# An expert MLP's second layer: three 256-column products become one of 512 columns and one of 256, with a PSUM bank for each tile

## The chip, the cores and the metric

The kernel runs on one core of a Trainium2 chip. TensorE is PE in the profile, and PEld its weight loads, which overlap the products; VectorE is DVE, ScalarE is ACT, GpSimd is POOL and SyncE, which issues most transfers, is SP. The metric is the device time of the whole kernel in microseconds (us).

## The reference, cut to what matters

The network routes each of 2048 tokens to two of eight experts, adds their gated sum to x, and then puts the result through a stencil step. Routing and stencil are not touched by the change.

```python
D, E, FF, TOPK = 256, 8, 1024, 2
...
hid = jax.nn.relu(jnp.einsum('nd,edf->nef', h_flat, exp_w1) + exp_b1)
eout = jnp.einsum('nef,efd->ned', hid, exp_w2) + exp_b2
y = jnp.einsum('ned,ne->nd', eout, combine)
return x + y.reshape(x.shape)
```

## The kernel before, in words

The (token, expert) pairs are sorted by expert into tiles of 128 rows, and the tiles into 23 slots, each with one expert: slot s is a single of one tile if s % 3 is 2 and a pair of two tiles otherwise (`width`). Slots 0 to 3 and 22 are written out, the 18 between them are a loop of six slots on each engine. Weights, inputs and buffers of odd and even slots are apart (`par`).

Every fp32 operand is split into a rounded half ("hi", type fp32r) and the rest ("lo"), and a product of two operands is the sum hi*hi + hi*lo + lo*hi; PARTS lists these three. For layer 2, `hid[:, par, 0]` and `hid[:, par, 1]` are the halves of the hidden values, and `w_split[:, 1, par, 0]` and `[..., 1]` those of the weights.

A slot goes through these steps; each engine has them in a fixed order, and semaphores hold the engines together.

- POOL gathers the rows, PE transposes them (`turn`, L911), ACT and VectorE make the halves (`split_h`, `low_h` at L1255).
- ACT and VectorE make the halves of the weights (`split_w1`, `low_w1` at L1243; `split_w2` at L566, `low_w2` at L1249).
- `layer1` (L935, L937, L942) on PE into banks 0 to 3; ACT adds the bias and applies relu (L586, L589), `high` rounds (L598), `low_hid` on VectorE gives the rest (L1268, L1272); for singles VectorE first adds two partial sums (`add_halves`, L1261).
- `layer2` on PE (L964): for each tile 8 blocks of 128 hidden values, three products of 256 columns each, 24 to a tile. Both tiles of a pair share bank 4 (even slots) or 5 (odd); only the last slot puts its second tile into the other of the two.
- `finish` on VectorE copies the destinations (L1282) and adds the bias while it moves the sum to y_sb (L1291; L1287 for the last slot's first tile). POOL scatters y_sb.

The order on PE is layer1(k+1), turn(k+2), layer2(k). The order on VectorE in step k is source(k+2), finish(k-2), low_w1(k+1), the work on slot k's hidden values with low_h(k+1) between, and low_w2(k). Behind the loop VectorE first prepares the stencil's grids (L1341 to L1354), and then comes finish(20), the last slot's hidden values and weights, finish(21) and finish(22).

layer2(k) waits for its weights' and hidden halves, and for y_ok to be s-1, which finish(k-2) sets: two banks take turns. The transposes use bank 6, or 7 in slot 1.

Of the kernel before, what the change touches and what calls it, by code (L numbers as in the profile page):

```python
# [7 lines left out]
ALU = mybir.AluOpType  # L8
# [7 lines left out]
P = 128  # L16
NB, T, D = 8, 256, 256
N = NB * T
NJ = N // P
KD = D // P  # L20
E, FF, TOPK = 8, 1024, 2
S_SUB, SE, SH = 32, 64, 128
FB = FF // P
ST = 256
TB = ST // P
# [20 lines left out]
def width(s):  # L46
    return 1 if s % 3 == 2 else TB


def first_col(s):  # L50
    return ROWS + s // 3 if s % 3 == 2 else 2 * (2 * (s // 3) + s % 3)


def cols_of_parity(s):
# [66 lines left out]
def moe_then_stencil(nc, x, ids, dt, exp_w1, exp_b1, exp_w2, exp_b2, a_grid, b_grid, small, consts, out):  # L121
# [4 lines left out]
    with ctx:  # L126
        def sb(name, shape, dt_=F32):
            return ctx.enter_context(nc.sbuf_tensor(name, shape, dt_))

        def sem(name):  # L130
            return ctx.enter_context(nc.semaphore(name))

        psum = ctx.enter_context(nc.psum_tensor("psum", [P, 8, 512], F32))
        banks = [psum[:, i, :] for i in range(8)]
# [11 lines left out]
        b2_all = sb("b2_all", [P, E, D])  # L146
# [9 lines left out]
        with ExitStack() as phase:  # L156
            def own(name, shape, dt_=F32):
                return phase.enter_context(nc.sbuf_tensor(name, shape, dt_))
# [3 lines left out]
            w_split = own("w_split", [P, 2, 2, 2, 2048], F32R)  # L162
            hid = own("hid", [P, 2, 2, FB, ST], F32R)
# [3 lines left out]
            y_sb = own("y_sb", [P, 2, TB, D])  # L167
# [150 lines left out]
        pool_go = sem("pool_go")  # L318
        part_ok = sem("part_ok")
        tr_done, y_ok = sem("tr_done"), sem("y_ok")  # L320
        l2_half, y_half = sem("l2_half"), sem("y_half")
        src_ok, dst_ok = sem("src_ok"), sem("dst_ok")
        rows_in = [sem(f"rows_in{i}") for i in range(2)]
# [27 lines left out]
        def field(g):  # L351
            return FV[0] if g == 0 else x_sb[:, 4 * g:4 * g + 4, :].rearrange("p j d -> p (j d)")
# [5 lines left out]
        def at_slot(k, m):  # L358
            return k if m is None else TURNS * m + (k - TURNS)
# [4 lines left out]
        def moved(k, m):  # L364
            per = 16 * cols_of_parity(TURNS - 1)
            return 16 * cols_of_parity(k) if m is None else per * m + 16 * cols_of_parity(k) - per
# [4 lines left out]
        def column(k, m):  # L371
            per = first_col(k + TURNS) - first_col(k)
            return first_col(k) if m is None else per * m + first_col(k) - per
# [103 lines left out]
        def _(act):  # L477
# [90 lines left out]
            def split_h(k, m):  # L568
                s, par, n = at_slot(k, m), k % 2, P * width(k)
                act.wait_ge(tr_done, s + 1)  # L570
                if k >= 2:
                    act.wait_ge(l1_done, BANKS * (s - 1))
                act.activation(slot_h[:, par, 0, :, 0:n],  # L573
                               banks[7 if k == 1 else 6].rearrange("p (k n) -> p k n", k=KD)[:, :, 0:n],
                               ACT.Copy).then_inc(h_hi, 1)

            def relus(k, m, bank):
# [51 lines left out]
            split_w1(0, None, first=True)  # L629
            split_w1(1, None, first=True)  # L630
            split_h(0, None)
            for k in range(FIRST):
                step(k, None)
# [40 lines left out]
            for g in range(NPAIR):  # L674
# [3 lines left out]
                for i in range(2):  # L678
# [6 lines left out]
                    else:  # L685
                        act.wait_ge(y2_added[g], 16)
                    last = act.activation(FD[g % 2][:, 512 * i:512 * i + 512], field(g)[:, 512 * i:512 * i + 512],
                                          ACT.Copy, scale=dt_b[:, 2 * g + i:2 * g + i + 1])
# [128 lines left out]
        def _(pe):  # L817
# [69 lines left out]
            for j in range(NJ):  # L887
                last = pe.matmul(banks[3][:, 0:E], ones_bf[:, :], m_bf[:, j, :], start=(j == 0), stop=(j == NJ - 1))
# [5 lines left out]
            for t in range(TOPK * NJ):  # L894
                if t % CHUNK == 0:
                    pe.wait_ge(ohrow_ok, t // CHUNK + 1)
                for part in range(2):
                    last = pe.matmul(banks[1][:, 128:128 + NC], oh_row[:, :, t], tok[:, part, :, t],  # L898
                                     start=(t == 0 and part == 0), stop=(t == TOPK * NJ - 1 and part == 1))
            last.then_inc(perm_mm, 1)  # L900

            def turn(k, m):
                s, par = at_slot(k, m), k % 2
                bank = 7 if k == 1 else 6
                pe.wait_ge(rows_in[par], moved(k, m))
                if k >= 2:
                    pe.wait_ge(h_hi, s)
                    pe.wait_ge(h_lo, s)
                for d in range(KD):
                    for t in range(width(k)):  # L910
                        last = pe.transpose(banks[bank][:, ST * d + P * t:ST * d + P * t + P],  # L911
                                            gathered[:, par, t, P * d:P * d + P], ident)
                last.then_inc(tr_done, 1)


            PARTS = ((0, 0), (0, 1), (1, 0))
# [32 lines left out]
            def layer2(k, m, halves=False):  # L949
                s, par = at_slot(k, m), k % 2  # L950
                pe.wait_ge(w2_hi, s + 1)
                pe.wait_ge(w2_lo, s + 1)
                pe.wait_ge(hid_lo, BANKS * (s + 1))
                if k >= 2:
                    pe.wait_ge(y_ok, s - 1)
                for t in range(width(k)):
                    bank = 4 + par
                    if halves and t == 1:
                        pe.wait_ge(y_ok, s)
                        bank = 5 - par  # L960
                    n = 0
                    for blk in range(FB):
                        for h, w in PARTS:
                            last = pe.matmul(banks[bank][:, D * t:D * t + D],  # L964
                                             hid[:, par, h, blk, P * t:P * t + P],
                                             w_split[:, 1, par, w, D * blk:D * blk + D],
                                             start=(n == 0), stop=(n == 3 * FB - 1))
                            n += 1
                    if halves and t == 0:
                        last.then_inc(l2_half, 1)  # L970
                last.then_inc(l2_done, 1)

            def step(k, m):
                layer1(k + 1, m)
                turn(k + 2, m)
                layer2(k, m)

            turn(0, None)
            layer1(0, None)
            for k in range(FIRST):  # L980
                step(k, None)
            with pe.Fori(1, ROUNDS + 1) as m:
                for k in range(FIRST, FIRST + TURNS):
                    step(k, m)
            layer2(NS - 1, None, halves=True)


# [40 lines left out]
        def _(dve):  # L1028
# [223 lines left out]
            def low_h(k, m):  # L1252
                s, par, n = at_slot(k, m), k % 2, P * width(k)
                dve.wait_ge(h_hi, s + 1)
                dve.tensor_tensor(slot_h[:, par, 1, :, 0:n],  # L1255
                                  banks[7 if k == 1 else 6].rearrange("p (k n) -> p k n", k=KD)[:, :, 0:n],
                                  slot_h[:, par, 0, :, 0:n].bitcast(F32), ALU.subtract).then_inc(h_lo, 1)

            def add_halves(k, m, bank):
# [16 lines left out]
            def finish(k, m, halves=False):  # L1276
                s, par, w = at_slot(k, m), k % 2, width(k)
                e = dve.value_load(e_idx[0:1, bass.DynSlice(s, 1)], min_val=0, max_val=E - 1)
                if k >= 2:
                    dve.wait_ge(y_out[par], moved(k - 2, m))  # L1280
                at = column(k, m)
                dve.tensor_copy(dst_cur[:, par, 0:w], dst_i[:, bass.DynSlice(at, w)]).then_inc(dst_ok, 1)  # L1282
                y = banks[4 + par].rearrange("p (t d) -> p t d", t=TB)
                t0 = 0
                if halves:
                    dve.wait_ge(l2_half, 1)
                    dve.tensor_tensor(y_sb[:, par, 0:1, :], y[:, 0:1, :], b2_all[:, bass.DynSlice(e, 1), :],  # L1287
                                      ALU.add).then_inc(y_half, 1)
                    y, t0 = banks[5 - par].rearrange("p (t d) -> p t d", t=TB), 1
                dve.wait_ge(l2_done, s + 1)  # L1290
                dve.tensor_tensor(y_sb[:, par, t0:w, :], y[:, t0:w, :],  # L1291
                                  b2_all[:, bass.DynSlice(e, 1), :].broadcast_to([P, w - t0, D]),
                                  ALU.add).then_inc(y_ok, 1)

            dve.wait_ge(rows_in[0], moved(0, None))
            low_w1(0, None)
            low_h(0, None)
            dve.wait_ge(rows_in[1], moved(1, None))
            low_w1(1, None)
# [45 lines left out]
            for at, cols in ((slice(0, 4), slice(0, 4)), (slice(4, 8), slice(D - 4, D))):  # L1345
                for n, gi, dst in ((0, 3, edge_w[:, 0, 0:KD, at]), (1, 1, edge_t[:, :, at]),
                                   (2, 4, edge_w[:, 1, 0:KD, at])):
                    last = dve.tensor_tensor(dst, grid[:, gi, :, cols], ew[:, n:n + 1, at].broadcast_to([P, KD, 4]),
                                             ALU.mult)
# [4 lines left out]
            dve.tensor_scalar(gr[:, 0:2, :], gr[:, 0:2, :], 0.5, None, ALU.mult).then_inc(grids_ok, 1)  # L1354

            finish(NS - 3, None)
            for bank in range(BANKS):
                low_hid(NS - 1, None, bank)
# [114 lines left out]
```

## Time and profile before

| | |
|---|---|
| median of 3 runs | 368.86 us (368.67 to 369.31) |
| span of the profiled execution | 368.1 us (368.07) |
| PE busy | 312.2 us, 85% of the span |
| VectorE busy | 286.2 us, 78% |
| ScalarE busy | 252.8 us, 69% |
| L964 (layer 2) on PE | 936 products, 117.8 us |
| mean granted TensorE clock | 0.944 |

The span is the time from the first to the last instruction of one profiled execution, and the runs were timed apart from it. Busy shares are means over stages with different limits: routing up to about 65 us, experts up to about 310, stencil behind that. A busy PE is not a PE at its peak, since consecutive products overlap in the records: how far apart they start counts, not how long one lasts.

### The profile page before, as it was taken

The numbers are of one execution on the slowest core, as the hardware profiler recorded it, in microseconds if no ns is written. First come the engines' busy times: TensorE is split into PE (matmuls) and PEld (weight loads), VectorE is DVE, ScalarE is ACT, GpSimd is POOL, SyncE is SP. The second block draws the span as 40 slices with busy tenths as digits, with TensorE's granted clock in tenths as the row PEclk, the third lists the DMA queues.
The fourth block names the chain that finished last, engine by engine and source line by source line (L and its number), as shares of the span: only waits on it lengthen the run. The fifth ranks groups of instructions, "written<-read, shape, count | busy, mean of one in ns | idle before, by whom it ended". The sixth has DMA issues, their size and how long they took to land.

```text
span 368.1 us, 7195 instructions
## 1 busy us (share of the span) xinstructions
PE 312.2 (85%) x2304; PEld 283.9 (77%) x2304; DVE 286.2 (78%) x517; ACT 252.8 (69%) x463; POOL 160.1 (44%) x114
## 2 busy tenths in 40 slices
PE   1757314789999999999999999999999996099996
PEld 1646314689999999999999999999999996034342
DVE  4988791688878878877886887887788692599993
ACT  2659014398899789789889978978988861197112
POOL 1445303152555654553554565455355414066540
PEclk9999855699999999999999999999999999579999
DMA  7902433894777875875877777576574400786513
GB/s 276 362 2 88 142 126 127 282 347 146 276 271 251 286 244 171 280 245 187 275 263 267 257 277 247 173 265 233 189 275 148 151 4 29 244 249 129 121 57 115
DMA packets 49780, 74.31 MB, mean 202 GB/s; under 512 B 3293, under 2 KB 40543, under 8 KB 49632
## 3 DMA queue, kind: packets, MB, share of 16 engines
q1 hardware_dynamic: 45056, 62.13, 49.6%
q0 software_dynamic: 4368, 11.54, 10.5%
q10 hardware_dynamic: 336, 0.39, 0.3%
q8 instruction: 10, 0.16, 0.2%
q14 instruction: 10, 0.08, 0.1%
HBM read 63.56 MB, written 9.31 MB: 198 GB/s over the span
## 4 chain that ended last, share of the span: by engine, by line
PE 72%; DVE 15%; DMA 6%; issue 2%; POOL 2%; ACT 1%; SPq 0%; DVEq 0%; POOLq 0%
PE psum L964 31%; PE psum L942 24%; PE psum L990 6%; PE psum L935 5%; PE psum L911 2%; DMA x_sb<-in_x_dram 2%; PE psum L937 2%; DMA raw_b<-in_L_cond_exp_w_dram 2%; PE psum L898 1%; DVE st L1072 1%; DMA t_y<-y_rows 1%; DVE z L1062 1%; POOL rs L722 1%; DVE t_b0f L1406 1%; PE psum L858 1%
## 5 line engine op out<-in xcount | busy, mean ns | idle before, releaser
L739 POOL DMA_INDIRECT gathered<-h_rows,src_cur x40 | 78.6, 1965 | 123.5 <-DVE src_cur L1238 66.1
L964 PE MATMUL psum<-w_split,hid 128*128 128x256 f32 x936 | 117.8, 285 | 0.2 <-issue 0.2
L964 PEld LDWEIGHTS psum<-w_split,hid 128*128 128x128 f32 x936 | 113.7, 192 | 0.3 <-issue 0.3
L942 PE MATMUL psum<-slot_h,w_split 128*128 128x256 f32 x768 | 96.5, 286 | 3.0 <-DVE slot_h L1255 3.0
L942 PEld LDWEIGHTS psum<-slot_h,w_split 128*128 128x128 f32 x768 | 94.7, 194 | 3.5 <-issue 3.5
L1249 DVE TENSOR_TENSOR w_split<-raw_b,w_split 128x2048 fp32r<-128x2048 f32 x23 | 52.7, 2293 | 22.3 <-ACT w_split L566 21.3
L589 ACT ACTIVATE relu<-psum,b_cur 128x256 f32<-128x256 f32 x128 | 53.6, 488 | 13.2 <-PE psum L942 10.9
L1243 DVE TENSOR_TENSOR w_split<-raw_a,w_split 128x2048 fp32r<-128x2048 f32 x23 | 52.5, 2282 | 8.1 <-DMA gathered<-h_rows,src_cur 7.0
L598 ACT ACTIVATE hid<-relu 128x512 fp32r<-128x512 f32 (+1 forms) x92 | 50.9, 588 | 9.6 <-DVE relu L1261 9.6
L752 POOL DMA_INDIRECT y_rows<-y_sb,dst_cur x39 | 43.1, 1106 | 27.1 <-issue 11.4
L1272 DVE TENSOR_TENSOR hid<-relu,hid 128x512 fp32r<-128x512 f32 x64 | 42.0, 687 | 10.0 <-ACT hid L598 9.4
L566 ACT ACTIVATE w_split<-raw_b 128x2048 fp32r<-128x2048 f32 x23 | 44.6, 1938 | 3.6 <-DMA raw_b<-in_L_cond_exp_w_dram 3.6
L559 ACT ACTIVATE w_split<-raw_a 128x2048 fp32r<-128x2048 f32 x23 | 44.7, 1945 | 2.6 <-DMA raw_a<-in_L_cond_exp_w_dram 2.6
L935 PE MATMUL psum<-slot_h,w_split 128*128 128x256 f32 x112 | 26.3, 332 | 0.0
L937 PE MATMUL psum<-slot_h,w_split 128*128 128x128 f32 x112 | 24.9, 223 | 0.0
L586 ACT ACTIVATE relu<-psum,b_cur 128x128 f32<-128x128 f32 x56 | 17.4, 363 | 7.7 <-PE psum L937 7.1
L937 PEld LDWEIGHTS psum<-slot_h,w_split 128*128 128x128 f32 x112 | 21.5, 192 | 0.0
L935 PEld LDWEIGHTS psum<-slot_h,w_split 128*128 128x128 f32 x112 | 21.1, 189 | 0.0
L1255 DVE TENSOR_TENSOR slot_h<-psum,slot_h 128x512 fp32r<-128x512 f32 (+1 forms) x23 | 14.0, 610 | 5.8 <-ACT slot_h L573 4.6
L911 PE MATMUL psum<-cst,gathered 128*128 128x128 f32 x80 | 13.2, 282 | 5.9 <-DMA gathered<-h_rows,src_cur 5.9
L846 PE MATMUL psum<-cst,z 128*128 128x128 f32 x32 | 8.5, 429 | 10.3 <-DVE z L1062 10.3
L573 ACT ACTIVATE slot_h<-psum 128x512 fp32r<-128x512 f32 (+1 forms) x23 | 12.8, 554 | 6.3 <-PE psum L911 6.3
(167 smaller groups left out, 357.4 us busy)
## 6 DMA issues: line engine op xcount, KB each, us to landing
raw_a<-in_L_cond_exp_w_dram SPq DMA_DIRECT2D x23, 1024.0 KB
raw_b<-in_L_cond_exp_w_dram SPq DMA_DIRECT2D x23, 1024.0 KB
t_y<-y_rows SPq DMA_DIRECT2D x6, 512.0 KB, 8.4
x_sb<-in_x_dram SPq DMA_DIRECT2D x4, 512.0 KB, 7.8
h_rows<-h_tok SPq DMA_DIRECT2D x16, 128.0 KB, 2.2
x_sb<-t_y POOLq DMA_DIRECT2D x4, 512.0 KB, 4.7
out_dram<-t_out SPq DMA_DIRECT2D x3, 512.0 KB, 2.9
b_all<-in_L_cond_exp_b_dram SPq DMA_DIRECT2D x1, 1024.0 KB, 10.5
```

The costliest lines, as they stand in the source:

```text
L559: act.activation(w_split[:, 0, par, 0, :], w1_raw[par], ACT.Copy).then_inc(w1_hi, 1)
L566: act.activation(w_split[:, 1, par, 0, :], w2_raw[par], ACT.Copy).then_inc(w2_hi, 1)
L589: last = act.activation(relu[:, bank, i, :], banks[bank][:, ST * i:ST * i + ST], ACT.Relu, bias=bias)
L598: act.activation(hid[:, par, 0, 2 * bank:2 * bank + 2, 0:n], relu[:, bank, :, 0:n], ACT.Relu if width(k) == 1 else ACT.Copy).then_inc(hid_ ...
L739: pool.indirect_dma_start(out=gathered[:, par, t, :], out_offset=None, in_=h_rows, in_offset=bass.IndirectOffsetOnAxis(ap=src_cur[:, par, ...
L752: pool.indirect_dma_start(out=y_rows, out_offset=bass.IndirectOffsetOnAxis(ap=dst_cur[:, par, t:t + 1], axis=0), in_=y_sb[:, par, t, :], i ...
L935: pe.matmul(both, w_split[:, 0, par, 0, at:at + P], slot_h[:, par, :, k, 0:P], start=(k == 0), stop=False)
L937: last = pe.matmul(both[:, 0, :], w_split[:, 0, par, 1, at:at + P], slot_h[:, par, 0, k, 0:P], start=False, stop=(k == KD - 1))
L942: last = pe.matmul(banks[bank][:, ST * (blk % 2):ST * (blk % 2) + rows], w_split[:, 0, par, w, at:at + P], slot_h[:, par, h, k, 0:rows], s ...
L964: last = pe.matmul(banks[bank][:, D * t:D * t + D], hid[:, par, h, blk, P * t:P * t + P], w_split[:, 1, par, w, D * blk:D * blk + D], star ...
L1243: dve.tensor_tensor(w_split[:, 0, par, 1, :], w1_raw[par], w_split[:, 0, par, 0, :].bitcast(F32), ALU.subtract).then_inc(w1_lo, 1)
L1249: dve.tensor_tensor(w_split[:, 1, par, 1, :], w2_raw[par], w_split[:, 1, par, 0, :].bitcast(F32), ALU.subtract).then_inc(w2_lo, 1)
```

## The change: what it does

The rounded half of hid meets both halves of the weights in one product of 512 columns, which fills a whole bank: hi*hi in its left half, hi*lo in its right. The product lo*hi of 256 columns goes into the left half. Each tile has a bank of its own: a pair of slot s takes banks 5 and 6 or 6 and 7, a single bank 5 (`out_bank`), and the transposes use bank 4, or 5 in slot 1 (`turn_bank`). layer2(k) waits for y_ok to be s, so for finish(k-1). In finish VectorE adds bias and left halves, waits for this, and adds the right halves.

```diff
+def out_bank(s):
+    return (5, 6, 5)[s % 3]
+
+
+def turn_bank(s):
+    return 5 if s == 1 else 4
...
+        y_left = sem("y_left")
...
-                bank = 7 if k == 1 else 6
+                bank = turn_bank(k)
...
-                if k >= 2:
-                    pe.wait_ge(y_ok, s - 1)
+                if k >= 1:
+                    pe.wait_ge(y_ok, s)
                 for t in range(width(k)):
-                    bank = 4 + par
-                    if halves and t == 1:
-                        pe.wait_ge(y_ok, s)
-                        bank = 5 - par
-                    n = 0
+                    out = banks[out_bank(k) + t]
                     for blk in range(FB):
-                        for h, w in PARTS:
-                            last = pe.matmul(banks[bank][:, D * t:D * t + D],
-                                             hid[:, par, h, blk, P * t:P * t + P],
-                                             w_split[:, 1, par, w, D * blk:D * blk + D],
-                                             start=(n == 0), stop=(n == 3 * FB - 1))
-                            n += 1
+                        pe.matmul(out.rearrange("p (w d) -> p w d", w=2), hid[:, par, 0, blk, P * t:P * t + P],
+                                  w_split[:, 1, par, :, D * blk:D * blk + D], start=(blk == 0), stop=False)
+                        last = pe.matmul(out[:, 0:D], hid[:, par, 1, blk, P * t:P * t + P],
+                                         w_split[:, 1, par, 0, D * blk:D * blk + D],
+                                         start=False, stop=(blk == FB - 1))
...
-                y = banks[4 + par].rearrange("p (t d) -> p t d", t=TB)
+                bias = b2_all[:, bass.DynSlice(e, 1), :]
+
+                def left(t0, t1):
+                    return dve.tensor_tensor(y_sb[:, par, t0:t1, :], psum[:, out_bank(k) + t0:out_bank(k) + t1, 0:D],
+                                             bias.broadcast_to([P, t1 - t0, D]), ALU.add)
+
+                def right(t0, t1):
+                    return dve.tensor_tensor(y_sb[:, par, t0:t1, :], y_sb[:, par, t0:t1, :],
+                                             psum[:, out_bank(k) + t0:out_bank(k) + t1, D:2 * D], ALU.add)
...
                 dve.wait_ge(l2_done, s + 1)
-                dve.tensor_tensor(y_sb[:, par, t0:w, :], y[:, t0:w, :],
-                                  b2_all[:, bass.DynSlice(e, 1), :].broadcast_to([P, w - t0, D]),
-                                  ALU.add).then_inc(y_ok, 1)
+                left(t0, w).then_inc(y_left, 1)
+                dve.wait_ge(y_left, s + 1 + t0)
+                right(t0, w).then_inc(y_ok, 1)
```

On PE, at the end of the loop and in the last slot, before:

```order
L964 MATMUL psum<-w_split,hid 128x256 [waits hid_lo,y_ok,w2_lo,w2_hi]
L964 MATMUL psum<-w_split,hid 128x256 x47
L982 REGISTER_ALU
L982 COMPARE_AND_BRANCH
L964 MATMUL psum<-w_split,hid 128x256 [waits hid_lo,y_ok,w2_lo,w2_hi]
L964 MATMUL psum<-w_split,hid 128x256 x23
L964 MATMUL psum<-w_split,hid 128x256 [waits y_ok]
L964 MATMUL psum<-w_split,hid 128x256 x23
```

The same place of the changed kernel, from the last products of the loop on:

```order
L970 MATMUL psum<-w_split,hid 128x256
L986 REGISTER_ALU
L986 COMPARE_AND_BRANCH
L968 MATMUL psum<-w_split,hid 128x512 [waits hid_lo,y_ok,w2_lo,w2_hi]
L970 MATMUL psum<-w_split,hid 128x256
```

The wait for y_ok in the middle of the last slot is gone, and the one at its start now asks for finish(21); 512 and 256 columns alternate 16 times.

On VectorE, behind the loop, from the last grid instruction to finish(21), before:

```order
L1354 TENSOR_SCALAR gr<-gr 128x1024
L1278 TENSOR_LOAD e_idx
L1278 ISA x2
L1282 COPY dst_cur<-dst_i 128x1 [waits y_out0]
L1291 ISA [waits l2_done]
L1291 TENSOR_TENSOR y_sb<-psum,b_all 128x256
L1272 TENSOR_TENSOR hid<-relu,hid 128x512 [waits hid_hi] x4
L1249 TENSOR_TENSOR w_split<-raw_b,w_split 128x2048 [waits w2_hi]
L1278 TENSOR_LOAD e_idx
L1278 ISA x2
L1282 COPY dst_cur<-dst_i 128x2 [waits y_out1]
L1291 ISA [waits l2_done]
```

The same place of the changed kernel, up to low_w2 (there L1253):

```order
L1368 TENSOR_SCALAR gr<-gr 128x1024
L1282 TENSOR_LOAD e_idx
L1282 ISA x2
L1286 COPY dst_cur<-dst_i 128x1 [waits y_out0]
L1290 ISA [waits l2_done]
L1290 TENSOR_TENSOR y_sb<-psum,b_all 128x256
L1294 TENSOR_TENSOR y_sb<-y_sb,psum 128x256 [waits y_left]
L1276 TENSOR_TENSOR hid<-relu,hid 128x512 [waits hid_hi] x4
L1253 TENSOR_TENSOR w_split<-raw_b,w_split 128x2048 [waits w2_hi]
```

Each finish has one instruction more, with a wait of its own, and none has changed its place.

## Rows read from the trace of the kernel before

**Rows 1.** Page: the chain by line, and the costliest group of PE's products

```profile
PE psum L964 31%; PE psum L942 24%; PE psum L990 6%; PE psum L935 5%; PE psum L911 2%; DMA x_sb<-in_x_dram 2%; PE psum L937 2%; DMA raw_b<-in_L_cond_exp_w_dram 2%; PE psum L898 1%; DVE st L1072 1%; DMA t_y<-y_rows 1%; DVE z L1062 1%; POOL rs L722 1%; DVE t_b0f L1406 1%; PE psum L858 1%
...
L964 PE MATMUL psum<-w_split,hid 128*128 128x256 f32 x936 | 117.8, 285 | 0.2 <-issue 0.2
```

**Rows 2.** Chain that ended last, in order of time: start us, us, what

```profile
199.93 5.76 PE psum L942 x48
```

**Rows 3.** Timeline of PE, several windows: start us, us, products merged

```profile
205.67 6.00 PE L964 MATMUL psum<-w_split,hid 128*128 128x256 f32 x48
...
227.49 3.12 PE L964 MATMUL psum<-w_split,hid 128*128 128x256 f32 x24
230.44 5.92 PE L942 MATMUL psum<-slot_h,w_split 128*128 128x256 f32 x48
...
68.80 2.55 PE L942 MATMUL psum<-slot_h,w_split 128*128 128x256 f32 x11
...
354.05 3.60 PE L990 MATMUL psum<-t_b0f,cst 128*128 128x512 f32 x8
...
359.20 3.17 PE L990 MATMUL psum<-t_u,cst 128*128 128x512 f32 x7
...
212.09 0.22 PE L937 MATMUL psum<-slot_h,w_split 128*128 128x128 f32 x1
212.15 0.33 PE L935 MATMUL psum<-slot_h,w_split 128*128 128x256 f32 x1
...
297.69 6.00 PE L964 MATMUL psum<-w_split,hid 128*128 128x256 f32 x48
303.86 5.98 PE L964 MATMUL psum<-w_split,hid 128*128 128x256 f32 x48 [0.18 <-issue]
```

**Rows 4.** Windows: us, PE busy (instructions), granted clock, DMA share, GB/s

```profile
69.00:71.00 2.00, 2.00 (x11) 0.50 1.09 353
```

**Rows 5.** Groups by form, windows 69:71 and 309.73:309.85: busy us, mean ns

```profile
L942 PE MATMUL psum<-slot_h,w_split 128*128 128x256 f32 x11 | 2.5, 415 | 0.0
...
L964 PE MATMUL psum<-w_split,hid 128*128 128x256 f32 x1 | 0.3, 279 | 0.0
```

**Rows 6.** Line L964: duration ns min/median/max, first and last start

```profile
L964 PE MATMUL psum<-w_split,hid x936: 278/283/365, 83.0 to 309.6; 128*128 128x256 f32 x188
```

**Rows 7.** Timeline of PEld in layer 1 of a single

```profile
212.09 0.19 PEld L935 LDWEIGHTS psum<-slot_h,w_split 128*128 128x128 f32 x1
212.20 0.19 PEld L937 LDWEIGHTS psum<-slot_h,w_split 128*128 128x128 f32 x1
```

**Rows 8.** Timeline of DVE, three slots: start us, us, [idle before <-releaser]

```profile
203.19 0.42 DVE L1291 TENSOR_TENSOR y_sb<-psum,b_all 128x256 f32<-128x256 f32 x1
...
222.45 0.68 DVE L1291 TENSOR_TENSOR y_sb<-psum,b_all 128x512 f32<-128x512 f32 x1
...
225.84 0.69 DVE L1272 TENSOR_TENSOR hid<-relu,hid 128x512 fp32r<-128x512 f32 x1 [0.51 <-ACT hid L598]
227.28 0.69 DVE L1272 TENSOR_TENSOR hid<-relu,hid 128x512 fp32r<-128x512 f32 x1 [0.75 <-ACT hid L598]
228.69 0.69 DVE L1255 TENSOR_TENSOR slot_h<-psum,slot_h 128x512 fp32r<-128x512 f32 x1 [0.71 <-ACT slot_h L573]
```

**Rows 9.** Timeline of DVE behind the loop

```profile
296.94 0.17 DVE L1351 TENSOR_TENSOR edge_w<-edge_w,edge_t 128x16 f32<-128x16 f32 x1
297.15 0.18 DVE L1352 COPY edge_w<-edge_w 128x32 f32<-128x32 f32 x1
...
297.57 0.69 DVE L1354 TENSOR_SCALAR gr<-gr 128x1024 f32<-128x1024 f32 x1
...
298.24 0.41 DVE L1291 TENSOR_TENSOR y_sb<-psum,b_all 128x256 f32<-128x256 f32 x1
...
301.46 2.29 DVE L1249 TENSOR_TENSOR w_split<-raw_b,w_split 128x2048 fp32r<-128x2048 f32 x1 [0.41 <-ACT w_split L566]
...
309.87 0.42 DVE L1291 TENSOR_TENSOR y_sb<-psum,b_all 128x256 f32<-128x256 f32 x1 [2.34 <-PE psum L964]
```

More of the change, by code:

```diff
@@ L573, in split_h @@
                 act.activation(slot_h[:, par, 0, :, 0:n],
-                               banks[7 if k == 1 else 6].rearrange("p (k n) -> p k n", k=KD)[:, :, 0:n],
+                               banks[turn_bank(k)].rearrange("p (k n) -> p k n", k=KD)[:, :, 0:n],
                                ACT.Copy).then_inc(h_hi, 1)
@@ L1255, in low_h @@
                 dve.tensor_tensor(slot_h[:, par, 1, :, 0:n],
-                                  banks[7 if k == 1 else 6].rearrange("p (k n) -> p k n", k=KD)[:, :, 0:n],
+                                  banks[turn_bank(k)].rearrange("p (k n) -> p k n", k=KD)[:, :, 0:n],
                                   slot_h[:, par, 0, :, 0:n].bitcast(F32), ALU.subtract).then_inc(h_lo, 1)
@@ L1286, in finish @@
                     dve.wait_ge(l2_half, 1)
-                    dve.tensor_tensor(y_sb[:, par, 0:1, :], y[:, 0:1, :], b2_all[:, bass.DynSlice(e, 1), :],
-                                      ALU.add).then_inc(y_half, 1)
-                    y, t0 = banks[5 - par].rearrange("p (t d) -> p t d", t=TB), 1
+                    left(0, 1).then_inc(y_left, 1)
+                    dve.wait_ge(y_left, s + 1)
+                    right(0, 1).then_inc(y_half, 1)
+                    t0 = 1
                 dve.wait_ge(l2_done, s + 1)
-                dve.tensor_tensor(y_sb[:, par, t0:w, :], y[:, t0:w, :],
-                                  b2_all[:, bass.DynSlice(e, 1), :].broadcast_to([P, w - t0, D]),
-                                  ALU.add).then_inc(y_ok, 1)
+                left(t0, w).then_inc(y_left, 1)
+                dve.wait_ge(y_left, s + 1 + t0)
+                right(t0, w).then_inc(y_ok, 1)
             dve.wait_ge(rows_in[0], moved(0, None))
```

## The prediction

> **What bounds the kernel now.** I read the page first: of the chain that ended last, 31% of the span are the second layer's products at L964 and 24% the first layer's at L942, both PE; PE sat idle for 0.2 us in all ahead of the 936 products of L964 [rows 1]. So the expert stage is TensorE's. In the chain, 48 products are a piece of 5.76 us, 120 ns each [rows 2], and PE's timeline shows the pieces of a stage end to end: 48 products of layer 2 from 205.67, 24 of a single from 227.49, layer 1 of the next slot from 230.44 [rows 3]. What shortens a product here shortens the kernel; what makes PE wait lengthens it. VectorE is the next engine, and its timeline tells when PE would have to wait for it.
>
> **What the change removes on PE.** A block was three products of 256 columns, 3 x 120 = 360 ns. It becomes one of 512 columns and one of 256, with one weight load less and as many columns as before (768). There are 23 slots, 7 singles of 8 blocks and 16 pairs of 16: 312 blocks. So everything hangs on how long 512 columns of this type take, which no row of before shows. From the nearest rows:
> - 256 columns are 120 ns apart. At half the granted clock (0.50, 1.2 GHz) [rows 4] 11 of them span 2.55 us [rows 3], with 415 ns for one [rows 5]: (2.55 - 0.415)/10 = 213 ns, one column per cycle. At 2.4 GHz that would be 106.7, so 13.3 ns of the 120 are something else.
> - The products of the last stage, 512 columns in two-cycle passes, are 3.60 us for 8 and 3.17 us for 7 [rows 3], 430 ns apart, some 3 above 1024 cycles. With no more surplus than that, 512 columns at one per cycle take about 216 ns: the lower bound.
> - In layer 1 of the singles a 128-column product starts at 212.09 and the next product at 212.15 [rows 3], so it holds the array 60 ns, half of 120. Read as a rate (0.47 ns per column), 512 columns take 240 ns and the change gives PE nothing: the upper bound.
> - The surplus of 13.3 ns as a fixed price of each product would make it 227; but then 128 columns would take 67, and they take 60.
> - The last product of the stage, with no weight load behind it, lasts 279 ns [rows 5], where the median is 283 [rows 6]: about 4 ns of the surplus go with the load that runs beside it. A load is about 110 ns long (two start at 212.09 and 212.20) [rows 7], so a 512-column product has one beside its first half only.
>
> I take the 128- and 256-column rows as the nearest, since they are of the same type, and let the second half go at the pace without a load: 120 for the first 256 columns, 116 for the rest, less some 2 ns for the start that is not paid twice: 234 ns. A block is then 234 + 120 = 354 against 360, a saving s of 6 ns (bounds 0 and 24).
>
> The Trainium skill ("TensorE: Matmul & The Clock Gate", Wait — 56ns, not 53.3ns?) puts consecutive warm products at N/2.4 GHz and about 2.5 ns more, 215.7 ns measured for 512 columns. By that rule a block would be 336 ns, s = 24; for 256 columns it gives 109, and the trace disagrees with 120.
>
> **What it adds on VectorE.** Each finish gets a second addition that waits for the first: 0.68 us for a pair, 0.42 for a single [rows 8], plus about 0.04 us between two dependent instructions (296.94 + 0.17 to 297.15) [rows 9]. In the steady part that is hidden by VectorE's idle time. The single's step is a train without gaps, so its extra addition and the next one's arrive together at the first pair's step, 1.5 us late; there VectorE waited 0.51, 0.75 and 0.71 us for ACT [rows 8], 1.97 in all, and the last of these three, low_h, is on time again. It ends at 228.69 + 0.69 = 229.38, and PE needs it at 230.44 [rows 3, 8]. Without that cover each late us past this last one would be PE's.
>
> **The wait that it tightens.** Layer 2 of slot k now waits for finish(k-1), not finish(k-2). On VectorE finish(k-1) stands right after low_w2(k), which layer 2 needed already. A finish that ended at 203.19 + 0.42 = 203.61 would end at 204.1, and the layer 2 that needs it starts at 205.67: 1.6 us of room. One that ended at 222.45 + 0.68 = 223.13 would end at 224.6, late and second addition together, against 227.49 [rows 3, 8]. Savings of 0.1 us per slot don't use that up. I cost the wait at nothing there.
>
> **At the end it is not hidden.** Two waits appear, one after another, on the chain that ends last.
> - Layer 2 of slot 21 started at 297.69 [rows 3]. It must now wait for finish(20), which VectorE does only after the grid work written ahead of it (its last is at 297.57): its addition runs at 298.24 for 0.41, the second ends at 298.65 + 0.04 + 0.42 = 299.11 [rows 9], and PE starts 0.11 later (as from low_w2's end, 301.46 + 2.29 = 303.75, to 303.86), at 299.2.
> - Layer 2 of slot 22 started at 303.86 [rows 3], held by low_w2 alone, since its first tile had a bank to itself. It must now wait for finish(21), which can't begin before slot 21's products are done. From the start of a pair's products to the addition behind them is 6.01 us (303.86 to 309.87) [rows 3, 9], here 6.01 - 16s: 305.21 - 16s. Then 0.69 + 0.04 + 0.69 + 0.11: PE starts at 306.74 - 16s.
> - Its own products and two additions of 0.42 follow: 306.74 + 6.01 + 0.42 + 0.04 + 0.42 = 313.63 - 32s, where before the last addition ended at 309.87 + 0.42 = 310.29 [rows 9]. low_w2, moved by 0.5 us, ends near 304 and holds nothing.
>
> All of this stands earlier by what slots 0 to 19 save, 14 pairs and 6 singles, 272 blocks; slot 20's 8 are lost, since VectorE's grid work follows layer 1 of slot 21 and not PE's later products. **The sum: +3.34 us - (272 + 32)s.** With s = 6 ns that is 3.34 - 1.82 = +1.5 us. Behind it nothing changes: scatter, loads of y and the stencil follow that last addition as before. The profiled execution's span was 368.07 us and the median of the runs is 368.86, 0.79 above; so 368.86 + 1.5 = **370.4 us**.
>
> **Rivals.**
> - *No gain on PE at all* (240 ns per 512 columns, by the exact 60 and 120): s = 0, +3.3 us, 372.2. Against it stand the 279 of the last product.
> - *A fixed surplus* (227): s = 13.3, 3.34 - 4.04 = -0.7, 368.2, no measurable change (0.2%, 0.74 us, is what a measurement of this kernel can tell). For it: the removed load is a plausible home of those ns. Against it: the 60 ns of 128 columns.
> - *The other side: the load is what stretches 256 columns.* A load takes some 110 ns and the columns 107; behind 512 columns it is hidden wholly, and the product takes 216, as the two-cycle passes suggest. s = 24 on every block, 3.34 - 7.3 = -4.0, 364.9. It decides from s = 13.5 on (a 512-column product under 226.5 ns). Against it: the last product, with no load behind it, is only 4 ns shorter, not 11. The rule of the page above is this rival's.
> - *A wait in the steady part.* If VectorE's train were 1.6 us later still, layer 2 of every first pair would stall; at half a us in each of seven turns that is 3.5 us on top, 373.9. The idle times above speak against it.
>
> **Chances.** Forecast (512 columns at 230 to 238 ns) 0.42; no gain 0.13; steady wait 0.05; fixed surplus 0.22; load hidden 0.18. So slower 0.60, same 0.22, faster 0.18. The forecast's own range is 369.2 to 371.6 (s from 10 to 2 ns). The range 366.5 to 372.8 adds the fixed surplus, with some 1.5 us below it, and the case without gain; it leaves out the hidden load and the steady wait.
>
> **What would show it.** The 512-column products last about 397 ns (234 and the 163 by which a record outlasts its pitch, 283 - 120), and the products of a pair take 5.66 us instead of 5.76. PE idles about 1.5 us ahead of slot 21's second layer and 1.8 ahead of slot 22's, released by VectorE's second addition, and nowhere else in the stage. The last addition ends 1.5 us later than 310.29. I am wrong if the 512-column records last 380 ns, if layer 2 waits for y_sb before 297 us, or if the two waits at the end are under 2.5 us together.

## The result, and the profile after

| | before | changed |
|---|---|---|
| median of 13 runs each, us | 368.86 (368.19 to 370.23) | 370.94 (369.97 to 372.61) |
| span of the profiled execution, us | 368.07 | 370.0 |
| PE busy, us | 312.2 | 309.9 |
| VectorE busy, us | 286.2 | 298.4 |

The ratio is 1.0050, with an interval of 1.0034 to 1.0066: slower, by 2.1 us. TensorE has less to do and the kernel takes longer, so there must be more idle time on TensorE; the question is what it waits for.

The page of the changed kernel, its first line, the chain by line, and the two groups that take the place of the one in [rows 1]:

```profile
span 370.0 us, 6596 instructions
...
PE psum L951 22%; PE psum L968 20%; PE psum L970 10%; PE psum L994 6%; PE psum L944 5%; PE psum L920 2%; DMA x_sb<-in_x_dram 2%; PE psum L946 2%; DMA raw_b<-in_L_cond_exp_w_dram 2%; DMA t_y<-y_rows 2%; PE psum L907 1%; DVE st L1076 1%; DVE z L1066 1%; POOL rs L731 1%; DVE t_b0f L1420 1%
...
L968 PE MATMUL psum<-w_split,hid 128*128 128x512 f32 x312 | 112.9, 404 | 3.2 <-DVE y_sb L1294 3.2
...
L970 PE MATMUL psum<-w_split,hid 128*128 128x256 f32 x312 | 87.6, 281 | 0.0
```

Layer 2 had 0.2 us of idle time ahead of its 936 products; now 3.2 us stand ahead of the 512-column ones, all ended by y_sb at L1294, VectorE's second addition. (Busy times of the two groups overlap and don't add up.) PE's waits between 72 and 316 us, the whole expert stage behind its start (us in total, times, longest), say that there are two of them:

```profile
PE psum L968 <- DVE y_sb L1294: 3.2, 2, 1.7
PE psum L951 <- DVE slot_h L1259: 0.4, 1, 0.4
```

PE's timeline has them both behind the loop, in front of slots 21 and 22; the first three rows are from the steady part:

```profile
205.33 0.40 PE L968 MATMUL psum<-w_split,hid 128*128 128x512 f32 x1
205.56 0.28 PE L970 MATMUL psum<-w_split,hid 128*128 128x256 f32 x1
205.68 0.40 PE L968 MATMUL psum<-w_split,hid 128*128 128x512 f32 x1
...
297.51 0.47 PE L968 MATMUL psum<-w_split,hid 128*128 128x512 f32 x1 [1.52 <-DVE y_sb L1294]
...
297.94 0.40 PE L968 MATMUL psum<-w_split,hid 128*128 128x512 f32 x1
...
302.79 0.40 PE L968 MATMUL psum<-w_split,hid 128*128 128x512 f32 x1
...
305.01 0.47 PE L968 MATMUL psum<-w_split,hid 128*128 128x512 f32 x1 [1.71 <-DVE y_sb L1294]
...
305.43 0.40 PE L968 MATMUL psum<-w_split,hid 128*128 128x512 f32 x1
...
309.32 0.40 PE L968 MATMUL psum<-w_split,hid 128*128 128x512 f32 x1
```

VectorE's timeline, the first three rows from the steady part (they answer to [rows 8]) and the rest from behind the loop ([rows 9]):

```profile
222.13 0.69 DVE L1290 TENSOR_TENSOR y_sb<-psum,b_all 128x512 f32<-128x512 f32 x1
222.85 0.69 DVE L1294 TENSOR_TENSOR y_sb<-y_sb,psum 128x512 f32<-128x512 f32 x1
...
227.36 0.69 DVE L1259 TENSOR_TENSOR slot_h<-psum,slot_h 128x512 fp32r<-128x512 f32 x1 [0.41 <-ACT slot_h L582]
...
295.70 0.69 DVE L1368 TENSOR_SCALAR gr<-gr 128x1024 f32<-128x1024 f32 x1
...
296.49 0.42 DVE L1290 TENSOR_TENSOR y_sb<-psum,b_all 128x256 f32<-128x256 f32 x1
296.95 0.42 DVE L1294 TENSOR_TENSOR y_sb<-y_sb,psum 128x256 f32<-128x256 f32 x1
...
303.45 0.69 DVE L1290 TENSOR_TENSOR y_sb<-psum,b_all 128x512 f32<-128x512 f32 x1 [1.39 <-PE psum L970]
304.18 0.69 DVE L1294 TENSOR_TENSOR y_sb<-y_sb,psum 128x512 f32<-128x512 f32 x1
...
311.39 0.42 DVE L1294 TENSOR_TENSOR y_sb<-y_sb,psum 128x256 f32<-128x256 f32 x1
```

Read the two timelines together. finish(20) stands behind the last grid instruction (295.70), its second addition ends at 297.37, and slot 21's products start at 297.51. finish(21) waits for slot 21's last product, its second addition ends at 304.87, and slot 22's products start at 305.01. The last addition of the stage ends at 311.81; before it ended at 310.29.

What PE gained on the way is read from the chain (start us, us, what). Layer 1 of the same slot, one turn of three slots later:

```profile
159.40 5.76 PE psum L951 x48
...
189.80 5.76 PE psum L951 x48
```

Three slots take 30.40 us. The same two pieces of the kernel before:

```profile
160.19 5.76 PE psum L942 x48
...
190.86 5.76 PE psum L942 x48
```

That is 30.67 us, so a turn's 40 blocks save 0.27 us, 6.75 ns each.

### The profile page after: what moved, and what is told of

It reads as the page before. It is cut to its first block, busy times and chain, and to the rows that moved or that the text cites. A ratio compares the mean times of both kernels' runs of the same rounds, so it can differ in the third digit from the quotient of the medians.

```text
span 370.0 us, 6596 instructions
## 1 busy us (share of the span) xinstructions
PE 309.9 (84%) x1992; PEld 266.8 (72%) x1992; DVE 298.4 (81%) x541; ACT 252.8 (68%) x463; POOL 150.8 (41%) x114
## 4 chain that ended last, share of the span: by engine, by line
PE 69%; DVE 17%; DMA 6%; issue 3%; POOL 2%; ACT 1%; SPq 1%; DVEq 0%; POOLq 0%
PE psum L951 22%; PE psum L968 20%; PE psum L970 10%; PE psum L994 6%; PE psum L944 5%; PE psum L920 2%; DMA x_sb<-in_x_dram 2%; PE psum L946 2%; DMA raw_b<-in_L_cond_exp_w_dram 2%; DMA t_y<-y_rows 2%; PE psum L907 1%; DVE st L1076 1%; DVE z L1066 1%; POOL rs L731 1%; DVE t_b0f L1420 1%
## 5 line engine op out<-in xcount | busy, mean ns | idle before, releaser
L748 POOL DMA_INDIRECT gathered<-h_rows,src_cur x40 | 63.8, 1594 | 130.2 <-DVE src_cur L1242 104.0
L968 PE MATMUL psum<-w_split,hid 128*128 128x512 f32 x312 | 112.9, 404 | 3.2 <-DVE y_sb L1294 3.2
L970 PE MATMUL psum<-w_split,hid 128*128 128x256 f32 x312 | 87.6, 281 | 0.0
L968 PEld LDWEIGHTS psum<-w_split,hid 128*128 128x128 f32 x312 | 58.6, 188 | 17.1 <-issue 3.7
L1253 DVE TENSOR_TENSOR w_split<-raw_b,w_split 128x2048 fp32r<-128x2048 f32 x23 | 52.7, 2292 | 20.2 <-ACT w_split L575 20.2
L761 POOL DMA_INDIRECT y_rows<-y_sb,dst_cur x39 | 48.7, 1248 | 31.1 <-DVE y_sb L1294 13.1
L970 PEld LDWEIGHTS psum<-w_split,hid 128*128 128x128 f32 x312 | 59.0, 189 | 0.0
L1290 DVE TENSOR_TENSOR y_sb<-psum,b_all 128x512 f32<-128x512 f32 (+1 forms) x24 | 14.0, 585 | 6.5 <-PE psum L970 6.5
```

The source lines that it names most:

```text
L748: pool.indirect_dma_start(out=gathered[:, par, t, :], out_offset=None, in_=h_rows, in_offset=bass.IndirectOffsetOnAxis(ap=src_cur[:, par, ...
L761: pool.indirect_dma_start(out=y_rows, out_offset=bass.IndirectOffsetOnAxis(ap=dst_cur[:, par, t:t + 1], axis=0), in_=y_sb[:, par, t, :], i ...
L968: pe.matmul(out.rearrange("p (w d) -> p w d", w=2), hid[:, par, 0, blk, P * t:P * t + P], w_split[:, 1, par, :, D * blk:D * blk + D], star ...
L970: last = pe.matmul(out[:, 0:D], hid[:, par, 1, blk, P * t:P * t + P], w_split[:, 1, par, 0, D * blk:D * blk + D], start=False, stop=(blk = ...
L1253: dve.tensor_tensor(w_split[:, 1, par, 1, :], w2_raw[par], w_split[:, 1, par, 0, :].bitcast(F32), ALU.subtract).then_inc(w2_lo, 1)
```

## The experiments

Every experiment is compared with runs of the kernel before on the same chip; its median there was 369.01 us for e1 to e4, 369.03 for e5 to e7 and 369.35 for e8 to e10. Since profiled spans differ by about 1 us for reasons that lie in front of and behind the experts, each trace is also read by its **expert stage**: from the start of layer 1's first product on PE to the end of the last addition on VectorE. Two profiles of one kernel (changed and e10) differ by 0.2 us in it.

| kernel | first product | last addition ends | stage, us | against before |
|---|---|---|---|---|
| before | 68.23 | 310.30 | 242.07 | |
| changed | 68.34 | 311.81 | 243.48 | +1.41 |
| e1 last slot's own banks | 68.97 | 310.53 | 241.56 | -0.51 |
| e2 finish(20) ahead of the grids | 67.48 | 310.06 | 242.58 | +0.51 |
| e3 both | 67.64 | 308.12 | 240.48 | -1.59 |
| e4 three products again | 67.38 | 312.94 | 245.56 | +3.49 |
| e5 one addition | 67.51 | 309.24 | 241.73 | -0.34 |
| e6 products grouped by width | 67.42 | 309.92 | 242.50 | +0.43 |
| e7 e3, last tile in the old form | 67.56 | 307.39 | 239.83 | -2.24 |
| e8 e7, grouped per tile | 67.43 | 306.34 | 238.92 | -3.15 |
| e9 e7, grouped over both tiles | 67.77 | 306.65 | 238.87 | -3.20 |
| e10 changed, again | 67.53 | 311.21 | 243.69 | +1.62 |

**e1: the last slot gets two banks of its own** (7 and 4), so that it needn't wait for finish(21).

```diff
+def last_bank(t):
+    return (7, 4)[t]
...
-                    pe.wait_ge(y_ok, s)
+                    pe.wait_ge(y_ok, s - 2 if halves else s)
...
-                    out = banks[out_bank(k) + t]
+                    out = banks[last_bank(t) if halves else out_bank(k) + t]
...
```

> The last slot's tiles get banks 7 and 4, which are free by then, so its products no longer wait for finish(21); the rest is the changed kernel. My theory (the loss is the two waits behind the loop, 1.5 and 1.7 us of idle PE in the trace of the changed kernel): the second wait goes and only low_w2 and slot 21's own products hold the last slot, so about 1.8 us less than the changed kernel, 369.1 us. Rival (the loss is VectorE's second additions in the steady part, and the waits at the end only stand in for others that would appear): within 0.5 us of the changed kernel's 370.9.

Measured 368.64, ratio 0.9992 (0.9976 to 1.0008). PE's waits of e1:

```profile
PE psum L972 <- DVE y_sb L1302: 1.5, 1, 1.5
PE psum L955 <- DVE slot_h L1263: 1.1, 1, 1.1
```

The longer wait is gone, the one ahead of slot 21 stays at 1.5 us, and the stage is 1.92 us shorter than the changed one, for a wait of 1.71; the other 0.2 us are within what two profiles of one kernel differ by. (The wait for slot_h is at the start of the stage, before the loop. It is 1.0 in the kernel before, 0.4 in the changed one and 0.7 in e10.)

**e2: finish(20) stands ahead of the grid work on VectorE.**

```diff
+            finish(NS - 3, None)
             dve.wait_ge(grid_in, 64)
...
-            finish(NS - 3, None)
```

> finish(20) stands ahead of the stencil's grid work on VectorE instead of behind it; the rest is the changed kernel. My theory: slot 21's products start 1.5 us earlier, but finish(21) then has to stand behind low_w2(22), which ends where it did, so slot 22's products start only about 1.4 us earlier: 369.5 us. Rival (steady part): within 0.5 us of 370.9.

Measured 368.87, ratio 1.0000 (0.9986 to 1.0014). PE's waits of e2:

```profile
PE psum L968 <- DVE y_sb L1294: 1.7, 1, 1.7
PE psum L920 <- DMA gathered<-h_rows,src_cur: 0.7, 1, 0.7
```

Now the other wait is left, 1.7 us. The stage is only 0.90 us shorter than the changed one, but that is not the edit's doing: this profile has 0.7 us of waiting for gathered rows near the stage's start, before the first product of layer 2. PE's timeline of e2 there, and below it that product in the changed kernel:

```profile
82.82 0.44 PE L920 MATMUL psum<-cst,gathered 128*128 128x128 f32 x2 [0.65 <-DMA gathered<-h_rows,src_cur]
83.02 0.48 PE L968 MATMUL psum<-w_split,hid 128*128 128x512 f32 x1
...
83.06 0.48 PE L968 MATMUL psum<-w_split,hid 128*128 128x512 f32 x1
```

From the first product of layer 2 to the last addition e2 takes 310.06 - 83.02 = 227.04 us and the changed kernel 311.81 - 83.06 = 228.75: 1.71 less, somewhat more than the wait of 1.5 that the edit removes. The +0.51 of the table is to be read with that.

**e3: e1 and e2 together.**

> Both edits, the last slot in banks 7 and 4 and finish(20) ahead of the grid work. My theory: neither wait is left, PE has at most 0.5 us of idle time ahead of the last slot (low_w2), 2.9 us less than the changed kernel, 368.0 us, so below the kernel before by about 0.9 us: what the products save (2.0 us) less the second addition that ends the stage and what low_w2 takes. Rival (steady part): no faster than the kernel before, 369 or more.

Measured 367.59, ratio 0.9958 (0.9943 to 0.9974). PE's waits of e3 have no y_sb at all:

```profile
PE psum L972 <- issue: 0.3, 1, 0.3
```

Without the two waits the change is what it looked like, a gain. Its size goes by the prediction's own terms: -304 x 6.75 ns + 0.46 for the second addition of the last finish = -1.59, and the stage has -1.59. That it fits to the last digit is luck, as two profiles of one kernel differ by 0.2 us.

**e4: the new banks, waits and additions, but three products of 256 columns**, hi*lo into the right half.

```diff
-                        pe.matmul(out.rearrange("p (w d) -> p w d", w=2), hid[:, par, 0, blk, P * t:P * t + P],
-                                  w_split[:, 1, par, :, D * blk:D * blk + D], start=(blk == 0), stop=False)
-                        last = pe.matmul(out[:, 0:D], hid[:, par, 1, blk, P * t:P * t + P],
-                                         w_split[:, 1, par, 0, D * blk:D * blk + D],
-                                         start=False, stop=(blk == FB - 1))
+                        for h, w in PARTS:
+                            last = pe.matmul(out[:, D * w:D * w + D], hid[:, par, h, blk, P * t:P * t + P],
+                                             w_split[:, 1, par, w, D * blk:D * blk + D],
+                                             start=(blk == 0 and h == 0 and w == 0), stop=(blk == FB - 1 and h == 1))
```

> The changed kernel's banks, waits and two additions, but each block again in three products of 256 columns (hi*hi and lo*hi into the left half of the bank, hi*lo into the right half). This is the sum with s = 0. My theory: the 304 blocks on the path give back 304 x 6.7 ns = 2.0 us, 372.9 us; by the forecast's own +3.3 us over the kernel before it would be 372.2. Rival (the 512-column products save nothing, and the changed kernel's loss is all there is): the same as the changed kernel, 370.9.

Measured 372.88, ratio 1.0100 (1.0080 to 1.0120). This is the cost of the change without its gain: +3.49 us in the stage, where the sum has +3.34 at s = 0. PE's waits, and the chain:

```profile
PE psum L969 <- DVE y_sb L1293: 3.2, 2, 1.7
```

```profile
159.15 5.76 PE psum L951 x48
...
189.82 5.76 PE psum L951 x48
```

The same two waits, and 30.67 us for three slots, as in the kernel before. So the new banks, waits and additions cost the loop nothing, and the 512-column product alone gives its 0.27 us per turn.

**e5: one addition per finish.**

```diff
...
-                left(t0, w).then_inc(y_left, 1)
-                dve.wait_ge(y_left, s + 1 + t0)
-                right(t0, w).then_inc(y_ok, 1)
+                left(t0, w).then_inc(y_ok, 1)
```

> The changed kernel without VectorE's second addition, so the product of hid's rounded half and the weights' low half is left out of the output; banks, products and waits are the same. My theory: the second additions cost only where PE waits for them, 0.46 us in finish(20), 0.73 in finish(21) and 0.46 in finish(22), together 1.65 us, so 369.3 us, and the steady part of three slots keeps its 30.40 us. Rival (VectorE's extra 15 us in the steady part hold PE or others up): more than 2.5 us less, below 368.4, and a shorter period.

Measured 368.41, ratio 0.9985 (0.9968 to 1.0002). Waits and chain of e5:

```profile
PE psum L968 <- DVE y_sb L1290: 1.9, 2, 1.0
```

```profile
158.61 5.76 PE psum L951 x48
...
189.01 5.76 PE psum L951 x48
```

Three slots still take 30.40 us: the second additions cost the steady part nothing. They cost at the end, where the two waits shrink from 3.2 to 1.9 us and the last finish has one addition less; the stage is 1.75 us shorter than the changed one, where the theory has 1.65. The median, 0.9 us below the theory's 369.3, stands at the edge of the rival's 368.4; what speaks against the rival is the unchanged turn.

**e6: within a tile first all eight 512-column products, then all eight of 256.**

```diff
+                    for blk in range(FB):
                         last = pe.matmul(out[:, 0:D], hid[:, par, 1, blk, P * t:P * t + P],
```

> The changed kernel with each tile's eight 512-column products first and its eight 256-column products behind them, the same work in another order. It tells where the saving of 6.7 ns per block lies. Forecast's reading (the second half of 512 columns goes without a load beside it): 512 columns 234 to 236 ns apart, 256 columns 120, a block 355, time within 0.7 us of the changed kernel. Rival 1 (a rate of 0.47 ns per column, and the alternation is what saves): 240 and 120, a block 360, about 2 us more, 372.9. Rival 2 (a fixed price of a product): 227 and 120, a block 347, about 2 us less, 368.9.

Measured 369.45, ratio 1.0014 (0.9992 to 1.0035); the stage is 0.98 us shorter than the changed one, with the 3.2 us of waits unchanged. Three slots take 30.23 us (layer 1 from 158.24 to 188.47 in its chain). The order of products alone is worth 0.17 us per turn. By the turn a block takes 349 ns, 11 less than with the old products: near rival 2's 347, and neither 355 nor 360.

**e7: e3, and the last slot's second tile has its three products of 256 columns in one half**, so that its finish needs one addition, and the semaphore between the two is not needed there.

```diff
+                        if halves and t == 1:
+                            for h, w in PARTS:
+                                last = pe.matmul(out[:, 0:D], hid[:, par, h, blk, P * t:P * t + P],
+                                                 w_split[:, 1, par, w, D * blk:D * blk + D],
+                                                 start=(blk == 0 and h + w == 0), stop=(blk == FB - 1 and h == 1))
+                            continue
...
+                if halves:
+                    left(t0, w).then_inc(y_ok, 1)
+                    return
```

> The kernel of both edits at the end (last slot in banks 7 and 4, finish(20) ahead of the grid work), and the last slot's second tile again in three products of 256 columns into one half, with one addition. My theory: the addition that ends the stage is 0.46 us shorter for 8 x 6.7 ns = 0.05 us of products, so 0.4 us less than without it, about 367.6 us, 1.3 us below the kernel before. Rival (steady part): no faster than the kernel before.

Measured 366.43, ratio 0.9926 (0.9902 to 0.9951). The stage is 0.65 us shorter than that of e3, where an addition and its start are 0.46 and 8 blocks' savings are lost. Most of the rest is not the edit's: in e7 slots 2 and 3, outside the loop, run at 347 ns a block and in e3 at 353, 0.15 us over their 24 blocks (see e10 on these two paces). The median moved by 1.2 us where the theory had 0.4; what is left of that is not accounted for.

**e8 and e9: e7, with the products grouped by width**, in e8 within a tile, in e9 over both tiles of a pair (e9's core is shown; wide(t, out) issues a tile's eight products of 512 columns, narrow(t, out) its eight of 256).

```diff
-                for t in range(width(k)):
-                    out = banks[out_bank(k) + t]
-                    for blk in range(FB):
...
+                    for t in range(width(k)):
+                        wide(t, banks[out_bank(k) + t])
+                    for t in range(width(k)):
+                        last = narrow(t, banks[out_bank(k) + t])
```

> The best kernel so far (last slot in banks 7 and 4, finish(20) ahead of the grid work, last tile in the old form) with each tile's 512-column products first and its 256-column products behind them. Theory after the grouped run (each product has a fixed surplus of 13 ns, and a 512-column product behind a 256-column one some 6 to 9 ns more): a block 347 to 348 ns instead of 353, over some 280 blocks 1.6 us less, 364.8 us. Rival (the stage is by now bound by VectorE or by the weights' loads, so faster products only wait): no change, 366.4, with waits of PE for w_split or slot_h.

> The same with the 512-column products of both tiles of a pair in a row and then the 256-column products of both. Theory (what is lost is at the change from 256 to 512 columns, some 15 ns, and there is one less to a pair): 15 pairs x 15 ns = 0.2 us less, 364.6 us, not to be told from the run with each tile apart. Rival (512 columns keep getting slower the longer they follow each other, since loads and reads of SBUF pile up): slower than that run by 0.5 us or more.

Measured 365.52, ratio 0.9904 (0.9883 to 0.9925), for e8, and 365.38, ratio 0.9886 (0.9868 to 0.9905), for e9: both beat the kernel before by some 4 us and the changed one by over 5. Against e7 the stage of e8 is 0.91 us shorter, where the theory had 1.6. Between e8 and e9 nothing can be told. PE's timeline of e9, a pair's layer 2, layer 1 of a single, and the 512-column products of the single's layer 2:

```profile
203.47 3.89 PE L971 MATMUL psum<-w_split,hid 128*128 128x512 f32 x16
207.19 2.08 PE L976 MATMUL psum<-w_split,hid 128*128 128x256 f32 x16
...
209.23 0.22 PE L950 MATMUL psum<-slot_h,w_split 128*128 128x128 f32 x1
209.29 0.34 PE L948 MATMUL psum<-slot_h,w_split 128*128 128x256 f32 x1
209.46 0.23 PE L950 MATMUL psum<-slot_h,w_split 128*128 128x128 f32 x1
209.52 0.33 PE L948 MATMUL psum<-slot_h,w_split 128*128 128x256 f32 x1
...
224.89 2.09 PE L971 MATMUL psum<-w_split,hid 128*128 128x512 f32 x8
```

The first 512-column product behind another stage holds PE for longer; with the 0.31 that it took in front of slot 21 of the changed kernel (297.51, and the 256-column product behind it at 297.82) and 0.40 for the last record, the others are (3.89 - 0.31 - 0.40)/14 = 227 ns apart. In the single the eight are (2.09 - 0.31 - 0.40)/6 = 230 ns apart. The 256-column ones are (2.08 - 0.28)/15 = 120 ns apart. Three slots take 30.19 us in e9's chain (158.55 to 188.74), 12 ns per block less than with the old products.

**e10: the changed kernel once more**, beside e8 and e9.

> The changed kernel, unaltered, beside the other two on one chip. Its expert stage, from the first transposes to the last addition, was 1.4 us longer than before in the profiled execution, while the median moved by 2.1. Theory (the 1.4 us and no more are the change's, the rest is the spread of the runs): 1.2 to 2.0 us over the kernel before, 370.4 to 371. Rival (the stage behind it has also become slower): 2.1 us or more again, with a profiled execution whose stencil stage is longer by half a us.

Measured 370.88, ratio 1.0037 (1.0021 to 1.0053), so 1.5 us slower this time, as the theory has it. (The part of the span behind the last addition is 0.4 us longer than in the kernel before; the rival had asked for half a us there and 2.1 in the median.) PE's timeline of e10, from the second 512-column product of slots 21 and 22 to the last:

```profile
297.34 0.40 PE L968 MATMUL psum<-w_split,hid 128*128 128x512 f32 x1
...
302.29 0.40 PE L968 MATMUL psum<-w_split,hid 128*128 128x512 f32 x1
...
304.93 0.40 PE L968 MATMUL psum<-w_split,hid 128*128 128x512 f32 x1
...
309.78 0.40 PE L968 MATMUL psum<-w_split,hid 128*128 128x512 f32 x1
```

Each piece is 14 blocks: 4.95 us or 354 ns a block in slot 21, 4.85 us or 346 ns in slot 22. In the first profile of the same kernel it is the other way round: 14 blocks of slot 21 from 297.94 to 302.79 are 346 ns each, 11 of slot 22 from 305.43 to 309.32 are 354.

## Why the prediction was right, and which of its reasons was not

**The two waits at the end: right, and shown.** 1.5 us was computed ahead of slot 21 and 1.52 is there, 1.8 ahead of slot 22 and 1.71. e1 and e2 take away one each and leave the other at its size; e3 takes both, and with them the loss. e4 measures everything but the saving: +3.49 us against +3.34.

**Nothing in the steady part: right.** No layer 2 waited for y_sb before 297 us. VectorE had waited 0.71 us ahead of low_h [rows 8] and still waits 0.41 there, so the late train is caught up by that point, as computed. e5 takes the additions away, and the turn stays at 30.40 us.

**The sum: right.** With the measured 6.75 ns in place of 6 it is 3.34 - 304 x 0.00675 = +1.29; the stage grew by 1.41 and 1.62 in two profiles, the last addition ends 1.52 us later, and the medians are 2.1 and 1.5 us apart. Behind the last addition, where the forecast has no change, the span has 57.8 us before and 58.2 in both profiles of the changed kernel; the other kernels have between 56.9 and 58.4. Whether these 0.4 us belong to the change or are spread isn't shown, nor where the 0.5 us come from by which the first median goes past the forecast.

**The step that failed: how long 512 columns take.** "let the second half go at the pace without a load: 120 for the first 256 columns, 116 for the rest, less some 2 ns ...: 234 ns". The number was near (a block of 353 against the 354 forecast), by luck: the reason was wrong. Behind their own kind 512 columns are 227 ns apart (e9), 14 more than 512 columns at one per cycle, and 256 columns are 120 apart, 13 more than theirs. So in a row of one kind the surplus comes once with each product, or with the weight load that each of these products has, and doesn't grow with the columns: the rival of the fixed surplus, which was given 0.22. By it a block is 347 ns, and e9's turn saves 12 ns per block of the 13 that it asks for.

What was held against that rival was "the 60 ns of 128 columns". e9's rows of layer 1, which the change doesn't touch, show the misreading: the 256-column product comes 60 ns behind the 128-column one, but the next 128-column one 170 ns behind that. The pair takes 230 ns for 384 columns, where the pace of 0.47 ns per column that I read from the 60 gives 180. One start-to-start distance in a train of two kinds is not the price of the first kind; only the whole turn is. Two weight loads of 110 ns [rows 7] would come near those 230, but that they set them is not shown. The other support of the 234, the 279 ns of the stage's last product, doesn't hold either: L964's shortest record, 278 ns [rows 6], is that of a product in the middle of the last slot, at 304.29.

The changed kernel's loop saves about half of those 13 ns: its two kinds of product alternate, and a block takes 353 ns. Alternating alone doesn't explain it, since in the slots outside the loop a block takes either 346 or 354, with the same code in the same order (e10 above), and 346 is what the fixed surplus asks for. So the forecast's 6 ns were the slower of two paces. What decides between them stays open, and so does where the 13 ns of each product come from. e6, e8 and e9 show a way around it: with the products grouped the loop is faster than any of the alternating ones.

The Trainium skill ("TensorE: Matmul & The Clock Gate", Wait — 56ns, not 53.3ns?) also has a fixed price per product, but of about 2.5 ns; no product of this type comes near it here: 227 ns against its 215.7 for 512 columns. The rival made from it (a block of 336 ns, 364.9 us) is refuted by e9, whose block is still some 12 ns above that. Nor is 336 what the rule gives: the prediction put the Trainium skill's 215.7 and the measured 120 together. By the Trainium skill's figures alone, as an estimate, a block would be 215.7 + 109 = 325 ns after three times 109, 327 to 328, before, so s would be some 2.5 ns, one fixed price, and the prediction's sum would give 371.4 us.

## What to carry to other kernels

When a change lets fewer buffers take turns, go through the loop's end slot by slot and ask what the releasing engine has written ahead of the release: the steady part had 1.6 us to spare, and the end paid 3.2 us for the same wait. Measure the price of a product in a run of its own kind, and write the products of one shape behind one another when they accumulate into the same place anyway. If a wait at the end eats the gain, give the last slots banks of their own and bring the releasing work forward before giving up the change: here that turned +0.5% into -0.4% (e3), and with the last tile in the old form and the products grouped it became -1.1% (e9).

## What the hardware showed that was not expected

- In a row of products of one kind and this type there are some 13 ns to each beside its columns, for 256 columns (120 ns) as for 512 (227 ns in e9's pairs; 230 in its singles, whose rows are half as long). At the lower granted clock (0.50, 1.2 GHz) it is not there: 213 ns for 256 columns [rows 3 to 5], one per cycle.
- 512 and 256 columns in turn run at one of two paces, 346 or 354 ns for both, for a whole slot; in the loop it was always the second. The first is close to the sum of 227 and 120, the second is some 7 ns more.
- Of 256 and 128 columns in turn, each with weights of its own, a pair takes 230 ns (layer 1 in e9), though the columns alone would take 160 at one per cycle.
